# Halves of the transition matrix made per graph by ScalarE and VectorE, and the last far low halves moved ahead of the variance, in layer 2 of a four-layer graph network

## The chip, the cores and the metric

One Trainium2 chip, one of its cores. The metric is the device time of one execution in microseconds (us), as a median over runs. The engines are TensorE (PE, matrix products; PEld is its weight load), VectorE (DVE), ScalarE (ACT), GpSimd (POOL) and SyncE (SP, which here only issues DMAs).

## The reference

64 graphs of 128 nodes with 256 features pass through four graph layers; each is followed by a residual and a layer norm. `x` is (64, 128, 256) and `adj` (64, 128, 128), both float32. The change concerns the third layer, called layer 2 in the kernel:

```python
Xw = X @ Wv + bv
sj = Xw @ aw[:d, 0]
si = Xw @ aw[d:, 0]
e = leaky_relu(sj[:, None, :] + si[:, :, None] + ab[0], negative_slope=0.2)
alpha_matrix = A * exp(e)
transition = alpha_matrix / (sum(alpha_matrix, axis=-1, keepdims=True) + 1e-12)
H = 0;  Xk = X
for k in range(3):
    H = H + Xk @ Wk[k] + bk[k]
    Xk = einsum('bij,bjd->bid', transition, Xk)
return relu(H)
# and around it: x = layernorm(x + layer2(x, adj))
```

## The kernel before

The kernel works on groups of four graphs, so each layer has 16 groups g. All of x stays in SBUF. Every engine has its own program, written out by hand as a fixed order of small steps; engines meet only in semaphores, so an instruction that waits holds back all that stands behind it on its engine. Layers overlap at seams, where steps of two layers take turns.

Matrix products of layer 2 are in float16 with two halves: a float32 tile v is kept as hi = f16(v) and lo = f16(v - hi), and `triple` issues three matmuls (lo by hi, hi by lo, hi by hi; lines 86, 87, 88).

For a group g, layer 2 does this:

- `project_near` and `project_far` on PE multiply the transposed halves of x (`xT_hi`, `xT_lo`) with the weights. Near is 512 columns wide (terms k=0 and k=1), far is 258 wide (term k=2 and the two score columns). `far_high` on ACT (line 1653) and `far_low` on DVE (line 1775) take far out of PSUM as halves, and `bias` (1659) takes out one score column.
- `spread` on PE (line 1593) spreads the other score column, ACT makes `t` (line 1646) and `e` = exp (line 1690).
- `transition` on DVE makes `u` = e times adjacency (1750), `row_sums` (1756 to 1760) the reciprocal row sums `rinv`, and `normalised` the float32 tile `tf` = u times rinv (1768). `T_high` on ACT (1684) copies `tf` to float16, `T_low` on POOL (1833) subtracts. SP transposes both halves by DMA into `TT_hi` and `TT_lo` (line 1530).
- `walk_far` on PE multiplies T with far, adding into near; `mid_high` (1678) and `mid_low` (1782) take the result out as halves; `walk_mid` multiplies once more; `add_bk` (1742) adds the bias into `hr`.
- `residual` (1733) adds x into `pre`, and four `norm_row` (bn_stats, line 1044) measure it. `norm_variance` on DVE (1051 to 1058) gives the variance. `norm_scales` on POOL makes the mean (1063, 1065), then from the variance `rstd` by a power of -0.5 (1069), then `nmr` (1072). `norm_apply` on ACT (1078) writes the new x.

Beside that, each step prepares the halves of x of two groups on: `x_high` on ACT (1123), `x_low` on POOL (1130), and SP transposes them by DMA (line 1144) into `xT_hi` and `xT_lo`. `project_far` and `project_near` of a group wait for both transposes.

Two orders matter below. POOL's step is `x_low(g+2)`, `T_low(g+1)`, `norm_scales(g)`; so `x_low` of a group stands right behind a `norm_scales`, which waits for a variance. DVE's step begins with `norm_variance(g-1)`, then the last two far low halves of the next group, then `mid_low`. PE's step is `walk_mid(g-1)`, three graphs of `project_near(g)`, `project_far(g+1)`, the fourth near, `walk_far(g)`, `spread(g+1)`.

Of the kernel before, what the change touches and what calls it, by code (L numbers as in the profile page):

```python
# [7 lines left out]
ALU = mybir.AluOpType  # L8
# [4 lines left out]
GP = 4  # L13
# [25 lines left out]
def upto(g, per, k):  # L39

    return g * per + k
# [996 lines left out]
def norm_row(L, dve, g, p, j, per=GP):  # L1038

    if j % (GP // per) == 0:  # L1040
        dve.wait_ge(L.pre_ok, upto(g, per, j // (GP // per) + 1))
    if j == 0 and reused(g, L.deep):
        dve.wait_ge(L.mean_ok, upto(g - L.deep, 2, 1))
    dve.bn_stats(L.st[p][:, j, :], L.pre[p][:, j, :]).then_inc(L.st_ok, 1)  # L1044


def norm_variance(L, dve, g, p, eps):

    dve.wait_ge(L.st_ok, upto(g, GP, GP))
    st = L.st[p]  # L1050
    dve.tensor_tensor(L.mdiff[:], st[:, :, 1], st[:, :, 4], ALU.subtract).then_inc(L.agg, 1)
    dve.scalar_tensor_tensor(L.m2[:], st[:, :, 2], eps * D, st[:, :, 5], ALU.add, ALU.add).then_inc(L.agg, 1)
    dve.wait_ge(L.agg, upto(g, 4, 1))
    dve.scalar_tensor_tensor(L.dd[:], L.mdiff[:], 0.25, L.mdiff[:], ALU.mult, ALU.mult).then_inc(L.agg, 1)
    dve.wait_ge(L.agg, upto(g, 4, 3))
    if reused(g, L.deep):
        dve.wait_ge(L.rstd_ok, upto(g - L.deep, 1, 1))
    dve.scalar_tensor_tensor(L.veps[p][:], L.m2[:], 1.0 / D, L.dd[:], ALU.mult, ALU.add).then_inc(L.agg, 1)  # L1058
# [420 lines left out]
def layer2(nc, K, ctx):  # L1479

    def sb(name, shape, dt=F32):
        return ctx.enter_context(nc.sbuf_tensor(f"l2_{name}", shape, dt))
# [8 lines left out]
    adjn, adj_in = K.adjn, K.adj_in  # L1491
    before_l2 = 8 * G
    rsum, reps, rinv = sb("rsum", [128, GP]), sb("reps", [128, GP]), sb("rinv", [128, GP])
    tf = sb("tf", [128, C])

    def halves(name, shape):
        return [sb(f"{name}_{s}", shape, F16) for s in ("hi", "lo")]
# [3 lines left out]

    far = [halves(f"far{p}", [128, GP, D + 2]) for p in range(2)]
    hr = sb("hr", [128, GP, D])
    rsum_ok, reps_ok, rinv_ok, tf_ok, t_hi, t_lo = map(
        sem, ("rsum_ok", "reps_ok", "rinv_ok", "tf_ok", "t_hi", "t_lo"))
    tT_in = [sem(f"tT_in{p}") for p in range(2)]
    far_ps, far_hi, far_lo, near_ps, mid_ps, mid_hi, mid_lo, out_ps, hr_ok = map(
        sem, ("far_ps", "far_hi", "far_lo", "near_ps", "mid_ps", "mid_hi", "mid_lo", "out_ps", "hr_ok"))
# [10 lines left out]
    def sync(sp):  # L1519
        def next_adj(g, p):  # L1520
            if reused(g):
                sp.wait_ge(S.u_ok, upto(g - 2, 1, 1))
                load_adj(K, sp, g, p)

        def transpose_T(g, p):
            for s in range(2):
                sp.wait_ge((t_hi, t_lo)[s], upto(g, 1, 1))
                if s == 0 and reused(g):
                    sp.wait_ge(out_ps, upto(g - 2, GP, GP))
                sp.dma_start(tT[p][s][:], ts[s][:], transpose=True).then_inc(tT_in[p], 16)  # L1530

        def step(g, p, has):
            if has(0):
                transpose_T(g, p)
            if halves_due(F, g + 2):
                transpose_x(F, sp, g + 2, p, (near_ps, GP))
            if has(2):
                next_adj(g + 2, p)
        return step, 2, 0
# [99 lines left out]
    def scalar(act):  # L1639
# [38 lines left out]
            act.activation(mid[j][0][:], b_near[j][:, 0:D], ACT.Copy).then_inc(mid_hi, 1)  # L1678

        def T_high(g, p):  # L1680
            act.wait_ge(tf_ok, upto(g, 1, 1))
            if reused(g, 1):
                turned(act, g - 1, 1 - p)
            act.activation(ts[0][:], tf[:], ACT.Copy).then_inc(t_hi, 1)  # L1684

        def exponentials(g):
            act.wait_ge(S.t_ok, upto(g, GP, GP))
# [37 lines left out]
    def vector(dve):  # L1725
# [19 lines left out]
        def transition(g, p):  # L1745
            dve.wait_ge(S.e_ok, upto(g, 1, 1))
            dve.wait_ge(adj_in[p], before_l2 + 8 * (g - p) + 16)
            if reused(g, 1):
                dve.wait_ge(tf_ok, upto(g - 1, 1, 1))
            dve.tensor_tensor(S.u[:], S.e[:], adjn[p][:].rearrange("p g n -> p (g n)"),  # L1750
                              ALU.mult).then_inc(S.u_ok, 1)

# [6 lines left out]
            dve.wait_ge(reps_ok, upto(g, 1, 1))  # L1759
            dve.reciprocal(rinv[:], reps[:]).then_inc(rinv_ok, 1)  # L1760

        def normalised(g):
            u = S.u[:].rearrange("p (g n) -> p g n", g=GP)
            dve.wait_ge(rinv_ok, upto(g, 1, 1))
            if reused(g, 1):
                dve.wait_ge(t_hi, upto(g - 1, 1, 1))
                dve.wait_ge(t_lo, upto(g - 1, 1, 1))
            dve.tensor_tensor(tf[:].rearrange("p (g n) -> p g n", g=GP), u,
                              rinv[:, :, None].to_broadcast([128, GP, N]), ALU.mult).then_inc(tf_ok, 1)

        def far_low(g, p, j):
            dve.wait_ge(far_hi, upto(g, GP, j + 1))
            if reused(g):
                dve.wait_ge(mid_ps, upto(g - 2, GP, j + 1))
            dve.tensor_tensor(far[p][1][:, j, :], b_far[j][:, 0:D + 2], far[p][0][:, j, :],
                              ALU.subtract).then_inc(far_lo, 1)
# [6 lines left out]

        def step(g, p, has):
            q = 1 - p
            if has(-1):
                norm_variance(L, dve, g - 1, q, EPS)
            if g == -3:
                far_low(0, 0, 0)
                far_low(0, 0, 1)  # L1790
                far_low(0, 0, 2)
                far_low(0, 0, 3)
            if has(1) and g >= 0:
                far_low(g + 1, q, 2)
                far_low(g + 1, q, 3)
            if has(0):
                mid_low(g, 0)
                mid_low(g, 1)
                mid_low(g, 2)
                mid_low(g, 3)  # L1800
                add_bk(g, 0)
                add_bk(g, 1)
                add_bk(g, 2)
            if g == -2:
                transition(0, 0)
                row_sums(0)
                normalised(0)
            if has(1) and g >= 0:
                transition(g + 1, q)
                row_sums(g + 1)  # L1810
                normalised(g + 1)
            if has(0):
                residual(g, p, 0)
                residual(g, p, 1)
                norm_row(L, dve, g, p, 0)
                add_bk(g, 3)
                norm_row(L, dve, g, p, 1)
                residual(g, p, 2)
            if has(2) and g > -2:
                far_low(g + 2, p, 0)  # L1820
                far_low(g + 2, p, 1)
            if has(0):
                residual(g, p, 3)
                norm_row(L, dve, g, p, 2)
                norm_row(L, dve, g, p, 3)
        return step, 3, 1

    def gpsimd(pool):
        def T_low(g, p):
            pool.wait_ge(t_hi, upto(g, 1, 1))  # L1830
            if reused(g, 1):
                turned(pool, g - 1, 1 - p)
            pool.tensor_tensor(ts[1][:], tf[:], ts[0][:], ALU.subtract).then_inc(t_lo, 1)  # L1833

        def step(g, p, has):
            q = 1 - p
            if halves_due(F, g + 2):
                x_low(K, F, pool, g + 2, p)
            if has(1):
                T_low(g + 1, q)  # L1840
            if has(0):
                norm_scales(K, L, pool, g, p)
        return step, 2, 0
# [226 lines left out]
```

## Time and profile before

| what | value |
|---|---|
| median of 3 runs | 676.03 us (675.19 to 676.68) |
| the profiled execution's own time | 676.46 us |
| its span, first to last instruction | 674.7 us |
| PE busy over the span | 622.4 us, 92% |
| DVE, ACT, POOL busy | 84%, 78%, 56% |
| layer 2's stretch 400 to 560 us: PE, DVE, ACT, POOL busy | 157.78, 143.84, 126.84, 68.07 of 160 us |

The profile is one execution. What lies between its span and its time, 1.8 us, is start and end of the program. Busy times of POOL are rough. A wait is charged to the last releaser that the records show. All 16 groups of layer 2 lie between about 378 and 570 us; from 400 on its steps follow each other evenly, one group per step.

### The profile page before, as it was taken

To read this page: it belongs to the slowest core of one execution; us is meant where nothing else is said; L and a number is where in the kernel's file an instruction comes from. 1 tells how busy PE (TensorE), PEld (TensorE's weight loads), DVE (VectorE), ACT (ScalarE), POOL (GpSimd) and SP (SyncE) were. 2 spreads that over 40 slices of the span, in tenths; PEclk is the share of its full clock that TensorE was granted. 3 is DMA by queue.
4 is the path that set the end of the run, shared out by engine and by line. 5 is a ranking of instruction groups with operands and counts; after the bars stand their busy time and mean duration, and the time that the engine had idled before them with its cause. 6 is when DMAs were issued, how large, how long until landed. Compare 5 with 4: busy or idle time off the path is not lost.

```text
span 674.7 us, 15857 instructions
## 1 busy us (share of the span) xinstructions
PE 622.4 (92%) x5014; PEld 451.5 (67%) x5014; DVE 564.2 (84%) x1712; ACT 525.5 (78%) x1191; POOL 378.5 (56%) x448
## 2 busy tenths in 40 slices
PE   5889999999999999779999979999999996999993
PEld 4567777777777776556666647665766663788882
DVE  3889998888888886769999889898988987588886
ACT  4667888877777777767888777787877885799995
POOL 1335556665555555746777434443435353799983
PEclk9999999999999999989999999999999999999998
DMA  9781439464636322544665334445454443477883
GB/s 272 185 223 48 83 65 229 83 149 86 146 83 165 78 33 32 93 95 83 92 95 107 65 64 94 97 93 96 94 102 88 102 88 64 80 182 187 185 185 126
DMA packets 174467, 76.14 MB, mean 113 GB/s; under 512 B 122161, under 2 KB 173873, under 8 KB 174385
## 3 DMA queue, kind: packets, MB, share of 16 engines
q1 hardware_dynamic: 164208, 66.34, 42.9%
q0 software_dynamic: 8448, 8.39, 8.6%
q8 instruction: 41, 0.67, 0.4%
q10 hardware_dynamic: 1728, 0.40, 0.3%
q14 instruction: 42, 0.34, 0.2%
HBM read 28.97 MB, written 8.39 MB: 55 GB/s over the span
## 4 chain that ended last, share of the span: by engine, by line
PE 26%; POOL 9%; DVE 8%; ACT 6%; DMA 5%; issue 4%; ACTq 0%; POOLq 0%; SPq 0%; DVEq 0%
PE banks L86 8%; PE banks L88 8%; PE banks L87 8%; POOL l_rstd L1069 4%; DMA xT_lo<-x_halves 3%; ACT x_resident L1078 3%; POOL x_halves L1130 3%; DVE l_st L1044 2%; DMA l_TT_lo<-l_T_lo 2%; POOL l_U L2036 2%; PE banks L1593 1%; ACT l_wexp L1293 1%; DVE l_wn L1362 1%; DVE l_pre L2005 1%; DVE l_veps L1058 1%
## 5 line engine op out<-in xcount | busy, mean ns | idle before, releaser
L1078 ACT ACTIVATE x_resident<-l_pre,l_nmr,l_rstd 128x256 f32<-128x256 f32 x256 | 140.7, 605 | 15.6 <-POOL l_nmr L1072 15.6
L973 POOL TENSOR_TENSOR hq<-hq 128x512 f32<-128x512 f32 x48 | 69.5, 1448 | 93.7 <-ACT hq L690 91.4
L1130 POOL TENSOR_TENSOR x_halves<-x_resident,x_halves 128x1024 f16<-128x1024 f32 x46 | 98.1, 2134 | 3.9 <-ACT x_halves L1123 3.2
L1044 DVE BATCH_NORM_STATS2 l_st<-l_pre 128x6 f32<-128x256 f32 x256 | 93.4, 410 | 0.0
L86 PE MATMUL banks<-Wk_lo,xT_hi 128*128 128x512 f16 (+1 forms) x256 | 83.5, 326 | 3.2 <-DVE l_pre L1327 1.8
L1069 POOL TENSOR_TENSOR l_rstd<-l_veps,minus_half 128x4 f32<-128x4 f32 x64 | 74.9, 1170 | 17.9 <-DVE l_veps L1058 14.2
L87 PE MATMUL banks<-Wk_hi,xT_lo 128*128 128x512 f16 (+1 forms) x256 | 83.3, 325 | 0.0
L88 PE MATMUL banks<-Wk_hi,xT_hi 128*128 128x512 f16 (+1 forms) x256 | 83.2, 325 | 0.0
L86 PE MATMUL banks<-W2T_lo,h_hi 128*128 128x257 f16 x256 | 70.3, 274 | 5.3 <-ACT zf L702 4.4
L88 PE MATMUL banks<-W2T_hi,h_hi 128*128 128x257 f16 x256 | 70.1, 274 | 0.0
L87 PE MATMUL banks<-W2T_hi,h_lo 128*128 128x257 f16 x256 | 70.1, 274 | 0.0
L677 ACT ACTIVATE hf<-banks,b_col 128x512 f32<-128x512 f32 x64 | 44.5, 696 | 26.9 <-PE banks L88 26.8
L839 DVE TENSOR_TENSOR h_lo<-hf,h_hi 128x512 f16<-128x512 f32 x64 | 42.8, 690 | 12.1 <-issue 8.2
L1833 POOL TENSOR_TENSOR l_T_lo<-l_tf,l_T_hi 128x512 f16<-128x512 f32 x16 | 18.5, 1158 | 58.7 <-ACT l_T_hi L1684 58.7
L1063 POOL TENSOR_TENSOR l_msum<-l_st 128x4 f32<-128x4 f32 x64 | 13.6, 213 | 66.7 <-DVE l_st L1044 66.2
L86 PE MATMUL banks<-xT_lo,W1T_hi 128*128 128x512 f16 x128 | 48.6, 379 | 1.8 <-DVE xT_lo L853 1.1
L1123 ACT ACTIVATE x_halves<-x_resident 128x1024 f16<-128x1024 f32 x46 | 48.4, 1052 | 1.9 <-DMA xT_lo<-x_halves 1.9
L88 PE MATMUL banks<-xT_hi,W1T_hi 128*128 128x512 f16 x128 | 48.5, 379 | 0.0
L87 PE MATMUL banks<-xT_hi,W1T_lo 128*128 128x512 f16 x128 | 48.5, 379 | 0.0
L86 PE MATMUL banks<-w_lo,xT_hi 128*128 128x1 f16 (+1 forms) x256 | 45.5, 221 | 3.2 <-ACT l_xw L1934 1.9
L87 PE MATMUL banks<-w_hi,xT_lo 128*128 128x1 f16 (+1 forms) x256 | 46.5, 220 | 0.0
L88 PE MATMUL banks<-w_hi,xT_hi 128*128 128x1 f16 (+1 forms) x256 | 46.5, 221 | 0.0
(200 smaller groups left out, 1933.7 us busy)
## 6 DMA issues: line engine op xcount, KB each, us to landing
adj<-in_adj SPq DMA_DIRECT2D x32, 256.0 KB, 3.4
x_halves<-in_x SPq DMA_DIRECT2D x16, 512.0 KB, 4.4
x_resident<-b_half SPq DMA_DIRECT2D x8, 1024.0 KB, 7.1
x_resident<-in_x POOLq DMA_DIRECT2D x16, 512.0 KB, 6.0
out<-x_resident SPq DMA_DIRECT2D x15, 512.0 KB, 3.2
x_resident<-in_L_gnn_W SPq DMA_DIRECT2D x2, 512.0 KB, 5.5
x_resident<-in_L_gnn_Wk SPq DMA_DIRECT2D x1, 768.0 KB, 9.4
xT_hi<-x_halves SPq DMA_TRANSPOSE x48, 3.2
```

The costliest lines, as they stand in the source:

```text
L86: nc.tensor.matmul(out, lhs[0], rhs[1], start=start, stop=False, **kw)
L87: nc.tensor.matmul(out, lhs[1], rhs[0], start=False, stop=False, **kw)
L88: return nc.tensor.matmul(out, lhs[0], rhs[0], start=False, stop=stop, **kw)
L677: act.activation(hf[:, h, :], b_hid[h % 2][:], ACT.Relu, bias=K.b1[:, h:h + 1], scale=1.0 / W_SCALE).then_inc(hf_ok, 1)
L839: dve.tensor_tensor(hs[1][:, h, :], hf[:, h, :], hs[0][:, h, :], ALU.subtract).then_inc(h_lo, 1)
L973: pool.tensor_tensor(hq[:, 0, :], hq[:, 0, :], hq[:, h, :], ALU.add).then_inc(hqs_ok, 1)
L1044: dve.bn_stats(L.st[p][:, j, :], L.pre[p][:, j, :]).then_inc(L.st_ok, 1)
L1069: pool.tensor_tensor(L.rstd[p][:], L.veps[p][:], K.minus_half[:], ALU.pow).then_inc(L.rstd_ok, 1)
L1078: act.activation(K.x[:, gcols(g, j)], L.pre[p][:, j, :], ACT.Identity, bias=L.nmr[p][:, j:j + 1], scale=L.rstd[p][:, j:j + 1]).then_inc(L. ...
L1123: act.activation(F.xs[p][0], x_group(K, g), ACT.Copy).then_inc(F.x_hi, 1)
L1130: pool.tensor_tensor(F.xs[p][1], x_group(K, g), F.xs[p][0], ALU.subtract).then_inc(F.x_lo, 1)
L1833: pool.tensor_tensor(ts[1][:], tf[:], ts[0][:], ALU.subtract).then_inc(t_lo, 1)
```

## The change

The float32 tile `tf` goes. ACT makes the high half of T straight from `u` in four instructions of 128 columns, one per graph, each with that graph's column of `rinv` as scale. DVE makes the low half in four instructions of the form u times rinv minus hi. POOL's `T_low` goes. On DVE the new `T_low` stands behind the first two residuals of the step. For the first group it stands a step later than the row sums. DVE's `norm_variance` moves from the front of the step to behind the two far low halves. The next group's `transition` now waits for the two halves of T instead of for `tf`.

```diff
-    tf = sb("tf", [128, C])
...
         def T_high(g, p):
-            act.wait_ge(tf_ok, upto(g, 1, 1))
+            act.wait_ge(rinv_ok, upto(g, 1, 1))
             if reused(g, 1):
                 turned(act, g - 1, 1 - p)
-            act.activation(ts[0][:], tf[:], ACT.Copy).then_inc(t_hi, 1)
+            for j in range(GP):
+                act.activation(ts[0][:, j * N:(j + 1) * N], S.u[:, j * N:(j + 1) * N], ACT.Copy,
+                               scale=rinv[:, j:j + 1]).then_inc(t_hi, 1)
...
-        def normalised(g):
-            u = S.u[:].rearrange("p (g n) -> p g n", g=GP)
-            dve.wait_ge(rinv_ok, upto(g, 1, 1))
...
-            dve.tensor_tensor(tf[:].rearrange("p (g n) -> p g n", g=GP), u,
-                              rinv[:, :, None].to_broadcast([128, GP, N]), ALU.mult).then_inc(tf_ok, 1)
+        def T_low(g, p):
+            if reused(g, 1):
+                turned(dve, g - 1, 1 - p)
+            for j in range(GP):
+                dve.wait_ge(t_hi, upto(g, GP, j + 1))
+                c = slice(j * N, (j + 1) * N)
+                dve.scalar_tensor_tensor(ts[1][:, c], S.u[:, c], rinv[:, j:j + 1], ts[0][:, c], ALU.mult,
+                                         ALU.subtract).then_inc(t_lo, 1)
...
         def step(g, p, has):
             q = 1 - p
-            if has(-1):
-                norm_variance(L, dve, g - 1, q, EPS)
...
             if has(1) and g >= 0:
                 far_low(g + 1, q, 2)
                 far_low(g + 1, q, 3)
+            if has(-1):
+                norm_variance(L, dve, g - 1, q, EPS)
...
                 row_sums(0)
-                normalised(0)
+            if g == -1:
+                T_low(0, 0)
             if has(1) and g >= 0:
                 transition(g + 1, q)
                 row_sums(g + 1)
-                normalised(g + 1)
             if has(0):
                 residual(g, p, 0)
                 residual(g, p, 1)
+            if has(1) and g >= 0:
+                T_low(g + 1, q)
...
     def gpsimd(pool):
-        def T_low(g, p):
-            pool.wait_ge(t_hi, upto(g, 1, 1))
-            if reused(g, 1):
-                turned(pool, g - 1, 1 - p)
-            pool.tensor_tensor(ts[1][:], tf[:], ts[0][:], ALU.subtract).then_inc(t_lo, 1)
...
-            if has(1):
-                T_low(g + 1, q)
             if has(0):
                 norm_scales(K, L, pool, g, p)
```

On VectorE, in a middle step of layer 2, this stood from the last two row statistics (`l_st`) to the second low halves before the change (`l_m` is the sum of the variances of a row's two halves, `l_veps` the variance):

```order
909 L1044 BN_STATS l_st<-l_pre 128x6 x2
910 L1051 TENSOR_TENSOR l_mdiff<-l_st 128x4
911 L1052 SCALAR_TENSOR_TENSOR l_m<-l_st 128x4
912 L1054 SCALAR_TENSOR_TENSOR l_dd<-l_mdiff 128x4
913 L1058 SCALAR_TENSOR_TENSOR l_veps<-l_m,l_dd 128x4
914 L1775 TENSOR_TENSOR l_far_lo<-banks,l_far_hi 128x258 x2
915 L1782 TENSOR_TENSOR l_mid_lo<-banks,l_mid_hi 128x256 x4
```

and this stands there now, with the variance's four instructions behind the two far low halves:

```order
909 L1044 BN_STATS l_st<-l_pre 128x6 x2
910 L1776 TENSOR_TENSOR l_far_lo<-banks,l_far_hi 128x258 x2
911 L1051 TENSOR_TENSOR l_mdiff<-l_st 128x4
912 L1052 SCALAR_TENSOR_TENSOR l_m<-l_st 128x4
913 L1054 SCALAR_TENSOR_TENSOR l_dd<-l_mdiff 128x4
914 L1058 SCALAR_TENSOR_TENSOR l_veps<-l_m,l_dd 128x4
915 L1783 TENSOR_TENSOR l_mid_lo<-banks,l_mid_hi 128x256 x4
```

The rest of the step is unmoved up to the row sums. Behind those, still on VectorE, the order before was (`l_tf` is the normalised tile):

```order
917 L1750 TENSOR_TENSOR l_u<-l_e,adj 128x512
918 L1756 TENSOR_REDUCE l_rsum<-l_u 128x4
919 L1758 TENSOR_SCALAR l_reps<-l_rsum 128x4
920 L1760 RECIPROCAL l_rinv<-l_reps 128x4
921 L1768 TENSOR_TENSOR l_tf<-l_u,l_rinv 128x512
922 L1733 SCALAR_TENSOR_TENSOR l_pre<-l_hr,x_resident 128x256 x2
923 L1044 BN_STATS l_st<-l_pre 128x6
```

and it is now, with the low half of T in four pieces behind the residuals:

```order
917 L1751 TENSOR_TENSOR l_u<-l_e,adj 128x512
918 L1757 TENSOR_REDUCE l_rsum<-l_u 128x4
919 L1759 TENSOR_SCALAR l_reps<-l_rsum 128x4
920 L1761 RECIPROCAL l_rinv<-l_reps 128x4
921 L1733 SCALAR_TENSOR_TENSOR l_pre<-l_hr,x_resident 128x256 x2
922 L1769 SCALAR_TENSOR_TENSOR l_T_lo<-l_u,l_rinv,l_T_hi 128x128 x4
923 L1044 BN_STATS l_st<-l_pre 128x6
```

On GpSimd, one step of before, from the low half of x to the next one:

```order
246 L1130 TENSOR_TENSOR x_halves<-x_resident,x_halves 128x1024
247 L1833 TENSOR_TENSOR l_T_lo<-l_tf,l_T_hi 128x512
248 L1063 TENSOR_TENSOR l_msum<-l_st 128x4
249 L1065 TENSOR_TENSOR l_mneg<-l_msum,minus_half 128x4
250 L1069 TENSOR_TENSOR l_rstd<-l_veps,minus_half 128x4
251 L1072 TENSOR_TENSOR l_nmr<-l_mneg,l_rstd 128x4
252 L1130 TENSOR_TENSOR x_halves<-x_resident,x_halves 128x1024
```

and the same stretch now, one instruction shorter and otherwise in the same order:

```order
249 L1130 TENSOR_TENSOR x_halves<-x_resident,x_halves 128x1024
250 L1063 TENSOR_TENSOR l_msum<-l_st 128x4
251 L1065 TENSOR_TENSOR l_mneg<-l_msum,minus_half 128x4
252 L1069 TENSOR_TENSOR l_rstd<-l_veps,minus_half 128x4
253 L1072 TENSOR_TENSOR l_nmr<-l_mneg,l_rstd 128x4
254 L1130 TENSOR_TENSOR x_halves<-x_resident,x_halves 128x1024
```

Only `T_low` has left: the low half of x still stands behind `l_rstd` and `l_nmr`.

## Rows read from the trace of the kernel before

**Rows 1.** Windows: busy us per engine with instruction counts, clock, DMA share.

```profile
400.00:560.00 160.00, 157.78 (x1140) 103.98 (x1137) 143.84 (x416) 126.84 (x329) 68.07 (x85) 1.00 0.47 94
```

**Rows 2.** Waits, 395 to 560 us: waiter, releaser, us in total, times, longest.

```profile
PE banks L86 <- DMA l_TT_lo<-l_T_lo: 2.4, 3, 1.3
PEld banks L86 <- DMA xT_lo<-x_halves: 2.3, 7, 0.5
```

**Rows 3.** Timeline of PE: start us, us, instruction. First far matmuls; one walk_far.

```profile
403.88 0.27 PE L86 MATMUL banks<-Wk_lo,xT_hi 128*128 128x258 f16 x1
...
481.74 0.27 PE L86 MATMUL banks<-Wk_lo,xT_hi 128*128 128x258 f16 x1
...
485.68 0.27 PE L86 MATMUL banks<-l_far_lo,l_TT_hi 128*128 128x256 f16 x1
...
492.63 0.27 PE L86 MATMUL banks<-Wk_lo,xT_hi 128*128 128x258 f16 x1
...
548.88 0.28 PE L86 MATMUL banks<-Wk_lo,xT_hi 128*128 128x258 f16 x1
```

**Rows 4.** Timeline of PE's weight loads, with idle time before and releaser.

```profile
448.16 0.10 PEld L86 LDWEIGHTS banks<-Wk_lo,xT_hi 128*128 128x128 f16 x1 [0.46 <-DMA xT_lo<-x_halves]
...
492.52 0.10 PEld L86 LDWEIGHTS banks<-Wk_lo,xT_hi 128*128 128x128 f16 x1 [0.22 <-DMA xT_lo<-x_halves]
```

**Rows 5.** Timeline of DVE in one step.

```profile
483.83 0.43 DVE L1775 TENSOR_TENSOR l_far_lo<-banks,l_far_hi 128x258 f16<-128x258 f32 x1 [0.17 <-ACT l_far_hi L1653]
...
485.29 0.17 DVE L1051 TENSOR_TENSOR l_mdiff<-l_st 128x4 f32<-128x4 f32 x1
...
485.69 0.16 DVE L1058 SCALAR_TENSOR_TENSOR l_veps<-l_m,l_dd 128x4 f32<-128x4 f32 x1
485.77 0.76 DVE L1775 TENSOR_TENSOR l_far_lo<-banks,l_far_hi 128x258 f16<-128x258 f32 x2
...
489.48 0.69 DVE L1750 TENSOR_TENSOR l_u<-l_e,adj 128x512 f32<-128x512 f32 x1 [0.33 <-ACT l_e L1690]
...
491.13 0.18 DVE L1760 RECIPROCAL l_rinv<-l_reps 128x4 f32<-128x4 f32 x1
491.34 0.69 DVE L1768 TENSOR_TENSOR l_tf<-l_u,l_rinv 128x512 f32<-128x512 f32 x1
```

**Rows 6.** Timeline of POOL in the same step.

```profile
485.93 1.01 POOL L1069 TENSOR_TENSOR l_rstd<-l_veps,minus_half 128x4 f32<-128x4 f32 x1
...
487.23 2.13 POOL L1130 TENSOR_TENSOR x_halves<-x_resident,x_halves 128x1024 f16<-128x1024 f32 x1
```

**Rows 7.** Timeline of SP's queue: transposes by DMA (us is the issue).

```profile
444.74 2.07 SPq L1144 DMA_TRANSPOSE xT_lo<-x_halves  x1
...
483.07 1.26 SPq L1530 DMA_TRANSPOSE l_TT_lo<-l_T_lo  x1
...
489.39 1.23 SPq L1144 DMA_TRANSPOSE xT_lo<-x_halves  x1
```

**Rows 8.** Timeline of ACT.

```profile
487.64 1.14 ACT L1646 ACTIVATE l_t<-banks,l_bias 128x128 f32<-128x128 f32 x4
...
490.79 0.59 ACT L1078 ACTIVATE x_resident<-l_pre,l_nmr,l_rstd 128x256 f32<-128x256 f32 x1
492.07 0.63 ACT L1684 ACTIVATE l_T_hi<-l_tf 128x512 f16<-128x512 f32 x1 [0.69 <-DVE l_tf L1768]
```

**Rows 9.** Timeline at the first group: DVE, POOL, SP's queue and PE.

```profile
390.59 1.46 DVE L1327 SCALAR_TENSOR_TENSOR l_pre<-l_vqk,banks,x_resident 128x256 f32<-128x256 f32 x1
...
394.27 1.08 DVE L1775 TENSOR_TENSOR l_far_lo<-banks,l_far_hi 128x258 f16<-128x258 f32 x3
...
390.61 1.16 POOL L1833 TENSOR_TENSOR l_T_lo<-l_tf,l_T_hi 128x512 f16<-128x512 f32 x1 [1.39 <-ACT l_T_hi L1684]
...
391.82 1.26 SPq L1530 DMA_TRANSPOSE l_TT_lo<-l_T_lo  x1
...
396.92 0.28 PE L86 MATMUL banks<-l_far_lo,l_TT_hi 128*128 128x256 f16 x1 [1.34 <-DMA l_TT_lo<-l_T_lo]
```

More of the change, by code:

```diff
@@ L1503, in layer2 @@
     hr = sb("hr", [128, GP, D])
-    rsum_ok, reps_ok, rinv_ok, tf_ok, t_hi, t_lo = map(
-        sem, ("rsum_ok", "reps_ok", "rinv_ok", "tf_ok", "t_hi", "t_lo"))
+    rsum_ok, reps_ok, rinv_ok, t_hi, t_lo = map(sem, ("rsum_ok", "reps_ok", "rinv_ok", "t_hi", "t_lo"))
     tT_in = [sem(f"tT_in{p}") for p in range(2)]
@@ L1526, in transpose_T @@
             for s in range(2):
-                sp.wait_ge((t_hi, t_lo)[s], upto(g, 1, 1))
+                sp.wait_ge((t_hi, t_lo)[s], upto(g, GP, GP))
                 if s == 0 and reused(g):
@@ L1748, in transition @@
             if reused(g, 1):
-                dve.wait_ge(tf_ok, upto(g - 1, 1, 1))
+                dve.wait_ge(t_hi, upto(g - 1, GP, GP))
+                dve.wait_ge(t_lo, upto(g - 1, GP, GP))
             dve.tensor_tensor(S.u[:], S.e[:], adjn[p][:].rearrange("p g n -> p (g n)"),
@@ L1760, in row_sums @@
             dve.reciprocal(rinv[:], reps[:]).then_inc(rinv_ok, 1)
-        def normalised(g):
-            u = S.u[:].rearrange("p (g n) -> p g n", g=GP)
-            dve.wait_ge(rinv_ok, upto(g, 1, 1))
+        def T_low(g, p):
             if reused(g, 1):
-                dve.wait_ge(t_hi, upto(g - 1, 1, 1))
-                dve.wait_ge(t_lo, upto(g - 1, 1, 1))
-            dve.tensor_tensor(tf[:].rearrange("p (g n) -> p g n", g=GP), u,
-                              rinv[:, :, None].to_broadcast([128, GP, N]), ALU.mult).then_inc(tf_ok, 1)
+                turned(dve, g - 1, 1 - p)
[4 more added lines that the diff above has]
+                                         ALU.subtract).then_inc(t_lo, 1)
         def far_low(g, p, j):
@@ L1814, in step @@
                 residual(g, p, 1)
+            if has(1) and g >= 0:
+                T_low(g + 1, q)
+            if has(0):
                 norm_row(L, dve, g, p, 0)
```

## The prediction

> **What bounds the kernel now.** I read the windows first. In layer 2's even stretch PE is busy 157.78 of 160 us at full clock [rows 1]: it sets the pace, and the question is what can make it wait. The list of waits names two transposes by DMA: PE waited 3 times, 2.4 us in all, for the low half of T, and its weight loads waited 7 times for the low half of the next x, at most 0.5 us [rows 2]. The reader should see how near both are to the edge. The first far matmul of a group starts at 481.74 and that of the next at 492.63 [rows 3], 10.89 us apart. Thirteen such periods, from 403.88 to 548.88 [rows 3], take 145.00, 11.15 us each. So a period without a stall is 10.89 and the mean stall 0.26.
>
> Then I followed backwards, by timelines, what the far matmul at 492.63 needed. Its weight load at 492.52 waited for `xT_lo` [rows 4]. That DMA was issued at 489.39 [rows 7], 3.13 us earlier, and it was issued when POOL's `x_low` had ended (487.23 + 2.13 = 489.36 [rows 6]). `x_low` stands on POOL behind `rstd`, which began at 485.93 [rows 6], right after DVE's `veps` ended at 485.69 + 0.16 = 485.85. The variance began at 485.29, behind the last two row statistics, and those stand behind the far low half of 483.83 [rows 5], which waited for far numbers of the matmuls that began at 481.74. That is a closed loop from one group's far matmuls to the next one's: 481.74, 483.83, 485.29, 485.93, 487.23, 489.39, 492.52, 492.63. It takes the same 10.89 us as PE's own work. It has 0.0 to 0.1 us to spare; the 7 waits of the weight loads say so too.
>
> **The variance's new place.** It now stands behind the two far low halves. Before they began at 485.77, 0.48 after the variance's start, and took 0.76 together [rows 5]. Two that follow each other start some 0.35 apart (0.43 long, less the overlap that makes a pair of them 0.76 and not 0.86), so the variance starts 0.70 later (0.76 at most). At 485.77 they waited for nothing; if one had to wait at 485.29, the loop would get longer still. For DVE this is a swap; `mid_low` begins where it did. But the loop gets all of it. `rstd` waits for `veps`, `nmr` and `x_low` are queued behind `rstd` on POOL, SP issues `xT_lo` when `x_low` is done, and PE's next far matmuls, with everything of PE behind them, wait for it. Behind `xT_lo` on SP stand the adjacency load and the transposes of T. `xT_lo` is now issued at 490.09 and off the queue at 491.32, and T's high half is ready at 492.70 [rows 8], so there is room for the load between. The loop becomes 10.89 + 0.70 less 0.0 to 0.1 of slack, 11.49 to 11.59; I take 11.55. A DMA that is late adds to it: the `xT_lo` issued at 444.74 took 2.07 us to issue [rows 7] and released the load at 448.16 [rows 4], after 3.42 instead of 3.13. Two of the 14 were like that, 0.6 us in all. The stalls for T's low half (2.4 us in all, the longest 1.3) fall into time that PE now waits anyway, since they lie ahead of the next far wait. So 13 periods cost 13 x (11.55 - 11.15) + 0.6 = +5.8 us. The ends: 13 x (11.49 - 11.15) = +4.4, and 13 x (11.65 - 11.15) + 1.5 = +8.0 with the 0.76 and more late DMAs.
>
> **The halves of T.** `tf`, one DVE instruction of 0.69, and the copy of 0.63 on ACT go; from 491.34 to 492.07 + 0.63 that was 1.36 us [rows 5, 8]. ACT can begin when `rinv` ends, 491.31, and was idle for 0.69 before the copy [rows 8]. Four pieces of 128 columns with a scale column are not in the trace. The nearest row is four of 128 columns with a bias column, 1.14 us [rows 8]; the other bound is four of 256 columns with scale and bias columns, 4 x 0.59 = 2.36 [rows 8]. I take 1.3, near the first, which has the same width. So the high half is ready within 0.1 us of where it was, the next DMA follows at the same distance, and nothing is gained. The bounds give -0.2 to +1.0 us per group on this chain.
>
> The Trainium skill, "VectorE: DVE Perf Modes", section "The TRN2 errata", speaks against the cut: ScalarE pays some 224 cycles in each instruction from SBUF, so tiles should be 512 elements or more. By its formula, an estimate of that page, one of 512 takes 0.61 us and four of 128 take 1.17. The row for one of 512 (0.63) agrees, the four were never run here, and the sum would move by 0.1 us a group, in idle time of ACT.
>
> DVE gives up 0.69 per group and takes four low halves of 128 columns. A quarter of 0.69 and the whole of it bound one (0.17 to 0.69); with the 0.43 of a 258-wide row [rows 5] I take 0.25, 1.0 in all, the last ending some 0.2 after ACT's fourth. So DVE runs 0.3 to 0.4 late there. This is gone by the far low half of 483.83, which sits behind a wait for ACT of 0.17 [rows 5], and by the later start of the next far products.
>
> **POOL and DVE side by side.** At the first group an `l_pre` on DVE, with two inputs in SBUF, took 1.46 us from 390.59 to 392.05, while POOL's `T_low` ran from 390.61 to 391.77 [rows 9]; it was held until POOL was through, plus about 0.28. The change takes this away at the first group (1.46 less a usual 0.48, 1.0 us; the 258-wide row has 0.43 [rows 5]) and a little in each step. But it also puts `x_low` where it hurts. It now runs from 487.93 to 490.06, and `u` (two inputs in SBUF) starts at 489.48 [rows 5]: by the same reckoning it ends at 490.06 + 0.28 + 0.27 for its second half of columns, 490.6, instead of 490.17, so T's chain is 0.45 later. PE reached `walk_far` 3.94 us behind the first far matmul (485.68 - 481.74 [rows 3]); in the new period it gets there 0.6 to 0.7 later, so 0.45 still fits, with 0.2 to spare. It costs nothing in the middle, and +0.4 at the last group, where no far matmul is left to wait for.
>
> The Trainium skill states this as a rule in "GPSIMD Engine Reference", section "Specifications": the two engines share their SBUF interfaces, and contend when the VectorE instruction has two SBUF inputs. The row of 1.46 agrees. Read alone, the rule would promise a gain from taking `T_low` off GpSimd; here most of GpSimd's work that collides is `x_low`, which stays.
>
> **The first group.** PE waited until 396.92 for a `TT_lo` issued at 391.82 [rows 9], 5.1 us. Now DVE makes this low half behind layer 1's variance, where far low halves began at 394.27 [rows 9]: less 0.61 for `tf` and 0.98 for the held `l_pre`, it starts at 392.7, ends at 393.5 and its DMA is issued at 393.55. With the 2.61 from the issue at 483.07 [rows 7] to `walk_far` at 485.68 [rows 3] PE starts at 396.15, so -0.8. If it again took 5.1, +1.7.
>
> **The sum** against the profiled execution: 676.46 + 5.8 + 0.4 - 0.8 = 681.9 us. That execution was 0.43 above the median of 676.03, so the median should be 681.5 us.
>
> **The rivals.**
>
> *The variance's delay is absorbed, and the kernel gets faster.* The point is PE's first far matmul. For the delay to be free `xT_lo` would have to land 3.13 - 0.70 = 2.4 us after its issue. For it: the waits on it are of weight loads, which run ahead, and PE itself lost little. Against: in seven groups the loads did wait, and at 448.16 PE started late. If so, stalls for T would also shrink, by the port: up to 2.4 us of them [rows 2], and 0.8 at the first group, 676.0 - 3.2 = 672.8 us. From a delay below 0.1 us it decides. Chance 0.12.
>
> *Absorbed, but T's chain gains nothing.* Then only the first group's 0.8 and the last one's 0.4 are left, 675.6 us. Chance 0.07.
>
> *T's chain becomes the bound.* If ACT's four pieces take 2.36, T's low half is 1.0 later, and 0.45 more where `x_low` holds `u`. Before, T's chain had no slack, its stalls are in the mean of 11.15: the period is then 11.15 + 1.0 at the utmost, and around 11.9 with pieces of 0.5. 676.0 + 13 x (11.9 - 11.15) - 0.4 = 685.4 us. For it: `u` and `x_low` collide in each step. Against: the 128-wide row at 1.14 for four. Chance 0.16.
>
> **How the numbers follow.** A measurement of this kernel tells about 0.2% from no change, 1.35 us. Forecast 0.65, with its own range of 679.5 to 684.0. Of its chance, and of T's chain, nearly all is slower. The first rival is faster, the second is within 0.2%. With what else may happen I say faster 0.12, same 0.08, slower 0.80. The range, 676.5 to 686.0, takes in T's chain and reaches down to no change; the faster rival is left out.
>
> **What would show it.** Right: in the middle of layer 2 first far matmuls 11.5 to 11.7 us apart; at each a wait of PE for `xT_lo` of 0.5 to 0.8, some 8 us in all where 13 groups had almost none; `rstd` about 1.4 us behind the last row statistic and not 0.7; `u` with 1.1 us and not 0.69; no waits of PE for T. Wrong: far matmuls at 10.9 to 11.1, or waits of PE for T that outweigh those for x, or `xT_lo` landing earlier than 3 us after its issue.

## The result and the profile after

| what | before | after |
|---|---|---|
| median of 4 runs | 675.61 us (675.01 to 676.68) | 683.03 us (682.85 to 686.48) |
| ratio, with its 95% interval | | 1.0088 [1.0053, 1.0123] |
| the profiled execution's own time | 676.46 us | 682.85 us |
| its span | 674.7 us | 680.9 us |
| mean granted clock of PE | 0.990 | 0.986 |

Slower, as forecast (681.5, range 676.5 to 686.0). The quotient of the two medians alone is 1.0110; it lies within the interval. The start of the page of the kernel after, busy us by engine:

```profile
span 680.9 us, 15937 instructions
...
PE 627.0 (92%) x5014; PEld 453.2 (67%) x5014; DVE 567.5 (83%) x1760; ACT 535.2 (79%) x1239; POOL 359.5 (53%) x432
```

POOL has lost 16 instructions and 19 us, and the kernel has gained 6.2 us of span. Where the time lies is read from the first far matmuls on PE's timeline, one per group, as in [rows 3]. Far(k) is that of the k-th group, counted from 0; each column is the time between two of them. The usual period is the value that most periods share: six of the 13 before and seven of the 13 after lie within 0.02 us of it, the others are longer or a little shorter.

| kernel | far(0) to far(2) | far(2) to far(15) | usual period in there | far(15) to the end |
|---|---|---|---|---|
| before | 25.20 | 145.00 | 10.89 | 125.8 |
| after | 27.32 | 148.77 | 11.33 | 126.0 |

So of 6.2 us, 3.8 lie in the even stretch, 2.1 in the first two groups, and 0.3 ahead of and behind layer 2's groups. PE's timeline of the kernel after, with the two rows that bound the stretch, one pair in the middle, and the longest-waiting `walk_far` of that part:

```profile
406.16 0.27 PE L86 MATMUL banks<-Wk_lo,xT_hi 128*128 128x258 f16 x1
...
509.41 0.27 PE L86 MATMUL banks<-Wk_lo,xT_hi 128*128 128x258 f16 x1
...
520.66 0.28 PE L86 MATMUL banks<-Wk_lo,xT_hi 128*128 128x258 f16 x1
...
536.64 0.28 PE L86 MATMUL banks<-l_far_lo,l_TT_hi 128*128 128x256 f16 x1 [0.56 <-DMA l_TT_lo<-l_T_lo]
...
554.93 0.28 PE L86 MATMUL banks<-Wk_lo,xT_hi 128*128 128x258 f16 x1 [0.15 <-DMA xT_lo<-x_halves]
```

The waits of the kernel after from 400 to 560 us (waiter, releaser, us in total, times, longest):

```profile
PEld banks L86 <- DMA xT_lo<-x_halves: 6.4, 10, 0.8
...
PEld banks L86 <- DMA l_TT_lo<-l_T_lo: 4.6, 4, 1.6
PE banks L86 <- DMA l_TT_lo<-l_T_lo: 2.7, 4, 1.1
...
PE banks L86 <- DMA xT_lo<-x_halves: 1.4, 6, 0.3
```

The weight loads now wait 6.4 us for `xT_lo` and not 2.3. Most of it PE's matmuls still cover with those already queued, so PE's own row has only 1.4: the far wait has to be read from the weight loads.

The waits for T's low half have not gone. [rows 2] begin at 395 us, and 1.34 of their 2.4 us stand at 396.92, in the first groups. From 400 to 560 us the kernel before has these:

```profile
PE banks L86 <- DVE l_far_lo L1775: 1.1, 2, 0.7
PE banks L86 <- DMA l_TT_lo<-l_T_lo: 1.1, 2, 0.9
```

```profile
463.88 0.10 PEld L86 LDWEIGHTS banks<-l_far_lo,l_TT_hi 128*128 128x128 f16 x1 [1.22 <-DMA l_TT_lo<-l_T_lo]
```

The two waits charged to `l_far_lo` (0.73 at 463.89 and 0.35 at 497.09) are of a `walk_far` too, and the weight loads of both are charged to `l_TT_lo`. So before, PE waited up to 2.2 us for T's low half in this stretch, in four steps, and now 2.7 us, again in four.

DVE in the step that follows the far matmul at 509.41, which answers to [rows 5]:

```profile
512.17 0.74 DVE L1044 BATCH_NORM_STATS2 l_st<-l_pre 128x6 f32<-128x256 f32 x2
512.83 0.74 DVE L1776 TENSOR_TENSOR l_far_lo<-banks,l_far_hi 128x258 f16<-128x258 f32 x2
513.49 0.15 DVE L1051 TENSOR_TENSOR l_mdiff<-l_st 128x4 f32<-128x4 f32 x1
...
513.88 0.16 DVE L1058 SCALAR_TENSOR_TENSOR l_veps<-l_m,l_dd 128x4 f32<-128x4 f32 x1
...
517.26 0.84 DVE L1751 TENSOR_TENSOR l_u<-l_e,adj 128x512 f32<-128x512 f32 x1 [0.42 <-ACT l_e L1690]
...
519.82 1.13 DVE L1769 SCALAR_TENSOR_TENSOR l_T_lo<-l_u,l_rinv,l_T_hi 128x128 f16<-128x128 f32 x4
```

POOL in the same step, beside [rows 6]:

```profile
514.12 1.01 POOL L1069 TENSOR_TENSOR l_rstd<-l_veps,minus_half 128x4 f32<-128x4 f32 x1 [0.64 <-DVE l_veps L1058]
...
515.42 2.13 POOL L1130 TENSOR_TENSOR x_halves<-x_resident,x_halves 128x1024 f16<-128x1024 f32 x1
```

SP's queue and the weight load that waits for it, beside [rows 7] and [rows 4]:

```profile
517.58 1.54 SPq L1144 DMA_TRANSPOSE xT_lo<-x_halves  x1
```

```profile
520.65 0.10 PEld L86 LDWEIGHTS banks<-Wk_lo,xT_hi 128*128 128x128 f16 x1 [0.57 <-DMA xT_lo<-x_halves]
```

This is the forecast's loop, link by link. From the far matmul to `mdiff` it took 485.29 - 481.74 = 3.55 us and takes 513.49 - 509.41 = 4.08. From there on the links are as they were: `rstd` 0.63 later (0.64), `x_low` 1.30 (1.30), the DMA's issue 2.16 (2.16), the load 3.07 (3.13), the matmul 0.01 (0.11). The sum is 11.25, in other steps 11.33. The growth is in the first link; of its 0.53 us, 0.17 came back in the last two in this step.

### The profile page after: what moved, and what is told of

It is laid out like the page before. It is cut to its first block, busy times and chain, and to the rows that moved or that the text cites. A ratio compares the mean times of both kernels' runs of the same rounds, so it can differ in the third digit from the quotient of the medians.

```text
span 680.9 us, 15937 instructions
## 1 busy us (share of the span) xinstructions
PE 627.0 (92%) x5014; PEld 453.2 (67%) x5014; DVE 567.5 (83%) x1760; ACT 535.2 (79%) x1239; POOL 359.5 (53%) x432
## 4 chain that ended last, share of the span: by engine, by line
PE 17%; POOL 11%; DVE 10%; DMA 9%; ACT 8%; issue 5%; SPq 1%; ACTq 0%; POOLq 0%; DVEq 0%
DMA xT_lo<-x_halves 6%; PE banks L86 5%; POOL l_rstd L1069 5%; PE banks L88 5%; PE banks L87 5%; POOL x_halves L1130 4%; ACT x_resident L1078 4%; DVE l_st L1044 3%; DMA l_TT_lo<-l_T_lo 3%; POOL l_U L2032 1%; ACT l_T_hi L1683 1%; SPq L1528 1%; PE banks L1591 1%; DVE l_u L1751 1%; ACT l_wexp L1293 1%
## 5 line engine op out<-in xcount | busy, mean ns | idle before, releaser
L86 PE MATMUL banks<-qkvT_lo,xT_hi 128*128 128x384 f16 x128 | 42.2, 330 | 3.6 <-DMA xT_lo<-x_halves 3.6
```

The lines of the kernel that those rows point to most:

```text
L86: nc.tensor.matmul(out, lhs[0], rhs[1], start=start, stop=False, **kw)
```

## The experiments

Seven kernels. The ratio is to the kernel before, run beside it. Middle and period come from each kernel's profile as in the table above.

| kernel | median us (runs) | ratio [95%] | far(0) to far(2) | middle | period |
|---|---|---|---|---|---|
| variance alone | 680.77 (12) | 1.0061 [1.0042, 1.0080] | 23.69 | 150.60 | 11.34 |
| T alone | 681.16 (8) | 1.0061 [1.0038, 1.0085] | 26.02 | 146.61 | 11.01 |
| after, first T low half early | 681.72 (6) | 1.0070 [1.0045, 1.0095] | 23.88 | 149.97 | 11.33 |
| after, variance between the far lows | 680.76 (11) | 1.0056 [1.0037, 1.0074] | 27.37 | 146.37 | 11.01 |
| after, variance two places later | 711.07 (4) | 1.0494 [1.0455, 1.0533] | 27.24 | 169.74 | 12.78 |
| T alone, first low half early | 679.71 (12) | 1.0036 [1.0014, 1.0059] | 25.03 | 146.55 | 11.01 |
| that, far low half ahead of a residual | 677.55 (12) | 1.0011 [0.999, 1.0032] | 24.80 | 145.55 | 10.89 |

The kernel before had a median of 676.84 beside the first four of them (24 runs) and 677.2 beside the last three (23 runs). The medians expected, in the table's order, were 679.5, 678, 680.7, 680, 703, 677.5 and 674 to 675. All seven came out longer, six of them by 0.8 to 3.6 us and the fifth by 8; what the kernels show is read from their periods and waits.

The middle and the first groups are from one execution each. No edit touches anything ahead of far(0), and yet far(0) stands at 378.6 us in one profile and at 380.8 in another. So a difference of a microsecond or two between two profiles, outside the usual period, is not safely the edit's.

**The variance alone.** The kernel before, with the variance behind the far low halves.

```diff
         def step(g, p, has):
             q = 1 - p
-            if has(-1):
-                norm_variance(L, dve, g - 1, q, EPS)
...
                 far_low(g + 1, q, 2)
                 far_low(g + 1, q, 3)
+            if has(-1):
+                norm_variance(L, dve, g - 1, q, EPS)
```

> The kernel before with one edit: on VectorE norm_variance stands behind the last two far low halves; T is made as before. Theory A (a closed loop from one group's first far matmul to the next, through the variance, rstd, x_low and the transpose of x): the middle periods become 11.3 us (10.9 plus 0.5 for the later variance, less 0.1 of slack), with the transposes of T late in every third or fourth step their mean is 11.4, so +3.8 us on 13 periods, 679.5 us, and the seam to layer 2 with PE's full clock as before. Rival B (the pieces of T are what costs): 676, periods of 11.15 as before.

Measured: the period of the kernel after, with nothing of the T change in it. PE's timeline:

```profile
519.77 0.28 PE L86 MATMUL banks<-Wk_lo,xT_hi 128*128 128x258 f16 x1 [0.27 <-DMA xT_lo<-x_halves]
...
531.08 0.28 PE L86 MATMUL banks<-Wk_lo,xT_hi 128*128 128x258 f16 x1 [0.25 <-DMA xT_lo<-x_halves]
```

The variance's place makes the longer period. The middle is even 1.8 us longer than in the kernel after, in this one execution. Its waits of PE for T's low half were 4.4 us there against 2.7, in the same four steps (1.88, 0.90, 0.99 and 0.60 against 1.10, 0.54, 0.49 and 0.56). So beside the delayed variance the T change may give something back, but it is not shown: the kernel after with the first T low half early has both edits as well, and it had 3.2 us of these waits and a middle of 149.97, and its ratio (1.0070) is not below that of the variance alone (1.0061).

**T alone.** The kernel after, with the variance back at the front of the step.

```diff
         def step(g, p, has):
             q = 1 - p
+            if has(-1):
+                norm_variance(L, dve, g - 1, q, EPS)
...
-            if has(-1):
-                norm_variance(L, dve, g - 1, q, EPS)
             if has(0):
                 mid_low(g, 0)
```

> The changed kernel with norm_variance back at the front of the step; T's halves are still made per graph on ScalarE and VectorE. Theory A: middle periods back at 10.9 to 11.2 (mean 11.15), all that is left of the loss is the first group with its stretch of PE at the lower clock, 2.3 us: 678. Rival B: 683 or more with periods of 11.4. Rival C (the lower clock comes with the changed variance or by chance, not with the first T_low): 675.5.

Measured: the period is not 10.89 but 11.01. PE's timeline, and the wait of the weight loads from 400 to 560 us:

```profile
519.64 0.27 PE L86 MATMUL banks<-Wk_lo,xT_hi 128*128 128x258 f16 x1
...
530.65 0.27 PE L86 MATMUL banks<-Wk_lo,xT_hi 128*128 128x258 f16 x1
```

```profile
PEld banks L86 <- DVE l_far_lo L1776: 3.9, 13, 1.1
```

A wait stands in 13 of the 14 steps: the fourth far product needs the PSUM bank that the first `far_low` empties, and that one is now late, since the four low halves of T stand ahead of it on DVE (1.62 us behind the first far matmul, at 521.26, where it was 1.51 before, 494.14 - 492.63). T alone costs time by itself, 146.61 against 145.00 in the middle, and 0.8 in the first groups.

**The first group's low half early.** The kernel after, with `T_low(0, 0)` right behind the first row sums.

```diff
                 row_sums(0)
-            if g == -1:
                 T_low(0, 0)
```

> The changed kernel with the first group's T_low right behind the row sums, ahead of layer 1's residuals, and nothing else. The first low half's transpose is issued near 392 instead of 393.9. Theory (the lower clock and the loss at the first group come from where the first T_low stands): PE keeps 2.4 GHz after 396, the first walk_far starts near 395.5, the first period 403.9 - 394.5 is about 9.4 instead of 11.7, so 680.7 us. Rival (the drop has another cause): clock 0.5 for some 6 us again and 683.

Measured: 3.4 us came back in the first groups (27.32 to 23.88). PE's clock is part of it. Windows of this kernel (us, busy by engine, then the granted clock, DMA share and GB/s):

```profile
396.00:400.00 4.00, 4.00 (x40) 3.29 (x38) 2.88 (x9) 3.50 (x12) 2.31 (x3) 1.00 0.51 83
```

The middle was 149.97, 1.2 longer than after. The period from far(2) to far(3) took 11.98 us. The second group's low halves now wait for ACT, whose four pieces stand behind four `norm_apply` and `x_high`, and the far low halves are queued behind them; PE waited 0.84 us at 406.14. By medians alone this kernel isn't told from the one after: their ratios' intervals overlap.

**The variance between the last two far low halves.** A dose of one half.

```diff
                 far_low(g + 1, q, 2)
-                far_low(g + 1, q, 3)
             if has(-1):
                 norm_variance(L, dve, g - 1, q, EPS)
+            if has(1) and g >= 0:
+                far_low(g + 1, q, 3)
```

> The changed kernel with norm_variance between the last two far low halves: half the shift. Theory A (a loop that takes the shift one to one beyond 0.1 of slack): variance 0.2 to 0.3 after its old place, middle periods of 11.0 to 11.1 where no transpose of T is late, mean 11.2, 680 us with the first group's loss still in. Rival D (a threshold: any far low half in front of the variance costs the whole): 683.

```profile
519.22 0.27 PE L86 MATMUL banks<-Wk_lo,xT_hi 128*128 128x258 f16 x1
...
530.23 0.27 PE L86 MATMUL banks<-Wk_lo,xT_hi 128*128 128x258 f16 x1
```

DVE between them:

```profile
522.98 0.15 DVE L1051 TENSOR_TENSOR l_mdiff<-l_st 128x4 f32<-128x4 f32 x1
```

The variance began 522.98 - 519.22 = 3.76 us behind the far matmul, and the period is 11.01. It is 11.01 with the variance at the front too (above), by the late `far_low`. So beside the T change this first part of the shift costs nothing more, and the rest costs 0.32. This kernel does not test the loop by itself: the late `far_low` would give 11.01 without it (its weight loads waited for `l_far_lo` in 11 steps).

**The variance two places later.** Behind `mid_low` of graphs 0 and 1, a larger dose.

```diff
-            if has(-1):
-                norm_variance(L, dve, g - 1, q, EPS)
             if has(0):
                 mid_low(g, 0)
                 mid_low(g, 1)
+            if has(-1):
+                norm_variance(L, dve, g - 1, q, EPS)
+            if has(0):
```

> The changed kernel with norm_variance still further back, behind the first two mid_low halves. These stand behind a wait for ACT, so the variance starts about 5.75 us behind the first far matmul instead of 4.08. Theory A (the loop takes the shift one to one): middle periods of 11.33 + 1.65 = 13.0 us, all PE waits for xT_lo, 13 x 1.6 = +21 us on the changed kernel, about 703. Rival D (a threshold, or the loss lies in T's chain): 683.

PE's timeline, DVE's between the two, and PE's waits from 400 to 560 us:

```profile
536.28 0.28 PE L86 MATMUL banks<-Wk_lo,xT_hi 128*128 128x258 f16 x1 [1.50 <-DMA xT_lo<-x_halves]
...
549.07 0.28 PE L86 MATMUL banks<-Wk_lo,xT_hi 128*128 128x258 f16 x1 [1.49 <-DMA xT_lo<-x_halves]
```

```profile
541.84 0.15 DVE L1051 TENSOR_TENSOR l_mdiff<-l_st 128x4 f32<-128x4 f32 x1
```

```profile
PE banks L86 <- DMA xT_lo<-x_halves: 16.2, 11, 1.7
```

Those first far matmuls wait 1.5 us for `xT_lo`. The variance begins 5.56 us behind the far matmul, 1.48 later than in the kernel after, and the period is 12.78, 1.45 longer. Against the kernel before this one is 4.9% slower. Over the kernel after the middle grew by 21.0 us, as expected; another 4.7 lie behind far(15) (130.7 against 126.0) and were in no expectation. They were not followed further.

**T alone, with the first low half early.** The kernel with T alone, and this:

```diff
                 row_sums(0)
-            if g == -1:
                 T_low(0, 0)
```

> The changed kernel with norm_variance at its old place and the first T_low right behind the first row sums: what is left is how T is made in the middle. Theory: the first group at the full clock as in e3 (first far matmul of group 1 to that of group 2 near 23.9 us behind the one of group 0), middle periods of 11.01 as in e2, where PE waits 0.12 in each step for the first far low half, which DVE makes late: about 677.5. Rival (T per graph costs nothing in the middle): periods of 10.89 and 675.5.

0.99 us came back in the first groups (26.02 to 25.03), nothing in the middle. Beside the second experiment's 1.0061 its ratio is 1.0036, an overlap of intervals. The wait for `far_low` is still there.

**The first far low half ahead of the residual of graph 2.** One more edit on the last one.

```diff
                 norm_row(L, dve, g, p, 1)
-                residual(g, p, 2)
             if has(2) and g > -2:
                 far_low(g + 2, p, 0)
+            if has(0):
+                residual(g, p, 2)
+            if has(2) and g > -2:
                 far_low(g + 2, p, 1)
```

> e6 with one swap on DVE: the next group's first far low half stands ahead of the third residual instead of behind it. PE's fourth far product reuses the bank that this instruction empties. Theory (the 0.12 us a step in e2 is this bank): PE's wait for l_far_lo goes, middle periods 10.89 where no transpose of T is late, mean 11.1, -1.5 us against e6, and with the first group's gain 674 to 675, at or a little below the kernel before. Rival (the 0.12 comes from T's own chain): 11.01 as in e6.

From 410 to 560 us the weight loads waited for `far_low` in one place, where with the T change alone they waited in nearly every step. The 0.7 in PE's own row is of a `walk_far` at 431.34, whose weight load was waiting for `l_TT_lo`: that is a late transpose and not this bank.

```profile
PE banks L86 <- DVE l_far_lo L1776: 0.7, 1, 0.7
...
PEld banks L86 <- DVE l_far_lo L1776: 0.2, 1, 0.2
```

```profile
516.52 0.27 PE L86 MATMUL banks<-Wk_lo,xT_hi 128*128 128x258 f16 x1
...
527.41 0.27 PE L86 MATMUL banks<-Wk_lo,xT_hi 128*128 128x258 f16 x1
```

The period is PE's own 10.89 again, and the time that of the kernel before (1.0011 [0.999, 1.0032]). The T change repaired in this way shows neither a cost nor a gain. No version was faster than the kernel before.

## Why the prediction was right, and which of its steps were not

**The bound and the sign: right.** The loop through variance, `rstd`, `x_low` and `xT_lo` was closed with 0.0 to 0.1 us to spare, and lengthening it lengthened every period. The distance from the far matmul to `mdiff`, read from the timelines, and the period stand so to each other:

| kernel | far matmul to `mdiff` | period | difference |
|---|---|---|---|
| before | 3.55 | 10.89 | 7.34 |
| T alone, early, far low half ahead | 3.56 | 10.89 | 7.33 |
| variance between the far lows | 3.76 | 11.01 | 7.25 |
| after | 4.08 | 11.33 | 7.25 |
| variance alone | 4.10 | 11.34 | 7.24 |
| variance two places later | 5.56 | 12.78 | 7.22 |

From `mdiff` on the loop takes 7.22 to 7.25 us, whatever stands ahead; this rests on the kernels with 4.08, 4.10 and 5.56, since 11.01 can be the late `far_low` as well. Where that sum stays under 10.89, PE's own work sets the period: the slack was 10.89 - 3.55 - 7.25 = 0.09. T alone lies outside, with the first low half early or not (3.54 and 11.01), which is how its other cause shows.

**The shift: 0.53, not 0.70.** I priced the two far low halves in full, at 0.70. The last two row statistics start 2.77 us behind the far matmul before and 2.76 after. This is their row of before:

```profile
484.51 0.75 DVE L1044 BATCH_NORM_STATS2 l_st<-l_pre 128x6 f32<-128x256 f32 x2
```

Before, `mdiff` began 0.78 behind them (484.51 to 485.29); it reads what the last one has just written. Now the far low pair starts 0.66 behind them (512.17 to 512.83), and `mdiff` 0.66 behind the pair (513.49): 1.32 for 0.78. With one far low half between them it is 0.99 (521.99 to 522.98, in the kernel with the variance between), so the first costs 0.21 and the second 0.33: part of the first stands in a gap that DVE left idle before. That the gap comes from reading a fresh result was not tried by itself. The period became 11.33 and not 11.55; 13 x (11.55 - 11.33) = 2.9 us less than forecast.

**"The stalls for T's low half fall into time that PE now waits anyway": wrong for most of them.** In the middle they were at most 2.2 us and are 2.7 (above); the 2.4 that I counted there took in the first group's 1.34. A far matmul must wait for `xT_lo` at its time, but `walk_far` comes 4 us behind it, and what PE loses there pushes the next far matmul out. Only about 0.26 of each is taken back, because the far matmul behind it then finds `xT_lo` there. The far matmul at 543.60 came 11.63 us behind that of 531.97: 0.56 of stall, 0.30 of loss over 11.33. The other three such periods (12.17, 11.61 and 11.57, with stalls of 1.10, 0.54 and 0.49) come out alike. The stalls come in every third or fourth step, those in which a transpose is late. SP's queue in such a step, where the ordinary `TT_lo` takes 1.26 to issue and this 2.25:

```profile
533.08 2.25 SPq L1528 DMA_TRANSPOSE l_TT_lo<-l_T_lo  x1
```

So the middle is 13 x (11.33 - 11.15) = +2.3 by the clean period, and 148.77 - 13 x 11.33 = 1.5 of stalls beside it; I had 0.6 of late DMAs. Together 3.8 against 5.8. Told the other way, the usual period cost 13 x (11.33 - 10.89) = 5.7, and what lay above it fell from 3.4 (145.00 - 13 x 10.89) to 1.5. With the variance alone it stayed at 3.2 (150.60 - 13 x 11.34), so this fall is not the longer period's doing by itself; one execution of each does not tell what it is.

**Four pieces on ACT and DVE: sizes right.** I had taken 1.3 and 1.0 us; the rows are

```profile
519.27 1.28 ACT L1683 ACTIVATE l_T_hi<-l_u,l_rinv 128x128 f16<-128x128 f32 x4
```

and 1.13 at 519.82 on DVE. T's low half was done at 520.95, while SP issued its transpose only at 521.81, behind that of the high half. It was so before: high half done at 481.80, low half issued at 483.07, 1.27 later, now 521.81 - 520.55 = 1.26. POOL had finished the low half at 483.04, when SP had just become free (481.83 + 1.19 = 483.02). Whoever makes the low half in that time is hidden behind SP, and this is why taking it off POOL gained nothing. The page "VectorE: DVE Perf Modes" of the Trainium skill, section "The TRN2 errata", advises tiles of 512 elements or more against a fixed cost in each instruction; four pieces at 1.28 against one of 0.63 agree, and it stayed off the bound as forecast. The third rival, T as the bound, needed 2.36.

**"DVE runs 0.3 to 0.4 late [...] gone by the far low half [...] behind a wait of 0.17": wrong.** The first far low half was 0.1 us late (1.62 behind the far matmul for 1.51), and the weight loads waited for it: the experiment with T alone lost 0.12 in each period by it, and the swap of two DVE instructions gave it back. In the kernel after it hid behind the longer wait for `xT_lo`, so the total does not show it.

**`u` held by `x_low`: right in mechanism, smaller in size.** `x_low` ended at 517.55 and `u` at 518.10, 0.55 later, as reckoned; `u` took 0.84 and not the 1.1 forecast, since `x_low` ended 0.29 us behind the start of `u` and not 0.58. "GPSIMD Engine Reference", section "Specifications", of the Trainium skill has the shared SBUF interfaces that this rests on. The trace agrees, and adds the price: `u` ended 0.55 us behind `x_low` (of its own 0.69), an `l_pre` of half its width 0.28 behind POOL's instruction (of 0.48). In the other steps of the kernel after `u` took 0.69 to 0.97, and with the variance two places later 2.43 in most steps (544.02 to 546.45, `x_low` having ended at 545.90, again 0.55).

**The first group: -0.8 forecast, +2.1 measured.** Its timing came out. DVE, SP's queue and PE of the kernel after, beside [rows 9]:

```profile
389.23 1.68 DVE L1327 SCALAR_TENSOR_TENSOR l_pre<-l_vqk,banks,x_resident 128x256 f32<-128x256 f32 x4
...
392.74 1.13 DVE L1769 SCALAR_TENSOR_TENSOR l_T_lo<-l_u,l_rinv,l_T_hi 128x128 f16<-128x128 f32 x4
```

```profile
393.90 1.19 SPq L1528 DMA_TRANSPOSE l_TT_lo<-l_T_lo  x1
```

```profile
394.47 0.28 PE L86 MATMUL banks<-Wk_lo,xT_hi 128*128 128x258 f16 x1 [1.96 <-DVE l_far_lo L1776]
...
396.35 0.40 PE L86 MATMUL banks<-l_far_lo,l_TT_hi 128*128 128x256 f16 x1 [1.05 <-DVE l_far_lo L1776]
...
402.27 0.38 PE L86 MATMUL banks<-Wk_lo,xT_hi 128*128 128x512 f16 x1
```

The hold of `l_pre` went (four of them in 1.68 us). The transpose was issued at 393.90, 0.35 later than forecast, and `walk_far` began at 396.35, 0.57 earlier than before; my number was 0.8. (Its wait is charged to `l_far_lo`; its weight load at 396.35 is charged to `l_TT_lo`.) But then PE worked at half its clock. Windows of the kernel after, of the one before, and of T alone, 396 to 402 (the last to 400), with the granted clock third from the end:

```profile
396.00:402.00 6.00, 5.65 (x31) 4.30 (x32) 2.98 (x8) 3.52 (x10) 0.36 (x1) 0.50 0.64 134
```

```profile
396.00:402.00 6.00, 5.08 (x42) 3.72 (x43) 4.17 (x10) 4.60 (x13) 1.86 (x1) 1.00 0.54 110
```

```profile
396.00:400.00 4.00, 2.68 (x15) 1.85 (x16) 1.80 (x5) 1.77 (x7) 2.08 (x2) 0.72 0.63 120
```

From `walk_far` to the next near matmul it took 402.27 - 396.35 = 5.92 us, against 3.08 before: 2.84 lost and 0.57 gained, and the rest of the step makes it 2.1. This term was in no rival. Nor is 2.1 a sure size for it: the kernel before had a T transpose of 5.1 us in this very stretch, and the variance alone, which makes T as before, took 23.69 and not 25.20; against that the first groups lost 3.6.

**Why the total came out all the same.** The terms were +5.8, +0.4 and -0.8. Measured they are +3.8 in the middle, +0.2 at the end (126.0 against 125.8), and +2.1 in the first groups, with 0.2 ahead of them, rounded: 6.2 in the span, 6.4 in the two profiled executions (682.85 - 676.46), where 5.4 was forecast. The middle came out 2 us too small, the first group 3 too large. The number is right partly by luck, by two errors that cancel. The sign is not: the variance alone is slower by 0.6% [0.42, 0.80].

**The signs I had named.** They were poor ones. Far matmuls came 11.33 apart and not 11.5 to 11.7; PE's own waits for `xT_lo` were 1.4 us and not 8; `rstd` began 1.21 us behind the end of the last row statistic (0.67 before) where I had 1.4; `xT_lo` landed after 3.07, as it should. And one sign of being wrong came true as I wrote it: PE's waits for T (2.7) outweigh its waits for x (1.4). In the weight loads it is the other way round (4.6 and 6.4). The loop is shown by the moved variance and the periods that followed it, not by these sums of waits.

**What stays open.** PE's clock fell in all four profiles with the late first `T_low` (after, T alone, and both with the variance moved within the kernel after), and in none of the five without. What starts the fall isn't settled: it began at about 395.4, behind a wait of 1.96 us and at the start of one of 1.05, but before the change PE had waited 1.85, 0.70 and 1.34 us there and was not slowed. The first groups of the kernel with the variance alone took 23.69 against 25.20 with the same T, so about 1.5 us there is not the edit's. A T transpose that landed late in the one and not in the other fits it, but was not traced to its cause.

## What to carry to other kernels

When the busiest engine is fed by a loop that has no slack, an instruction moved ahead of a link of that loop costs what it delays that link, less the slack, once in every period. Follow the period backwards from the matmul to the matmul and see which instructions lie on it before reordering anything. Price a swap by the start-to-start distances on both sides, not by the busy times, and count each wait ahead of a matmul as lost unless it stands in front of the very wait that sets the period.

## What the runs showed of the hardware

- PE's granted clock was 0.50, the 1.2 GHz level, from 396 to 402 us at layer 2's start, behind a wait of 1.96 us and during and behind one of 1.05; in T alone the clock of 396 to 400 was 0.72. "TensorE: Matmul & The Clock Gate" of the Trainium skill, section "Part 1: The HAM clock gate", states those two levels, the lower for an engine found idle; the rows show them here in an otherwise busy kernel, at a cost of 2.8 us.
- A VectorE instruction with two inputs in SBUF that starts while GpSimd's `x_low` runs ends a fixed time behind it: `u`, 0.69 us alone, ended 0.55 us behind, whether it took 0.84 (at 517.26) or 2.43 (at 544.02, with the variance two places later).
- DMA transposes of T were late in every third or fourth step. The high half of T of a step at 531.84 landed after 4.1 us where others took 2.4, and a transfer of the instruction queue lay in that stretch and none in the step before. That the one causes the other was not tried.
- Of two ScalarE or VectorE instructions that follow each other, the second starts before the first ends: four VectorE instructions of 345 ns took 1.13 us, four of ScalarE of 387 ns (the median of all) took 1.28.
